# A context of 192 channels as a tile of 128 and a doubled tile of 64, with both ends of a fused transformer block reordered

## The reference

```python
B, N, D, H, DH, DC = 4, 512, 256, 16, 64, 192
def _attn(xq, ctx, wq, wkv, wo, bo):
    q = _heads(xq @ wq)
    k, v = jnp.split(ctx @ wkv, 2, axis=-1)
    q, k = _rope(q), _rope(_heads(k))
    a = jax.nn.softmax(jnp.einsum('bhnd,bhmd->bhnm', q, k) * DH ** -0.5, axis=-1)
    o = jnp.einsum('bhnm,bhmd->bhnd', a, _heads(v))
    return merge(o) @ wo + bo
attn_in = _adaln(x, cond, ...)
x = _attn(attn_in, attn_in, sa_wq, sa_wkv, sa_wo, sa_bo) + x
x = _attn(_adaln(x, cond, ...), _ln(context), ca_wq, ca_wkv, ca_wo, ca_bo) + x     # context: 192 channels
h = gelu(_adaln(x, cond, ...) @ ff_w1 + ff_b1)
x = h @ ff_w2 + ff_b2 + x
```

## Time and profile before

| | before |
|---|---|
| median of 3 runs | 1115.08 us (1114.47 to 1115.96) |
| profiled execution | 1118.88 us, its span 1117.1 us |
| TensorE matmul busy | 1097.2 us of the span (98%) |
| DVE, POOL, ACT busy | 858.1, 775.7, 636.9 us |
| mean granted TensorE clock | 0.994 of full speed |

### The profile page before, as it was taken

The page is one execution under the profiler, slowest core; times in us unless marked ns, Lnnn a source line. Parts: engine busy times, 40 slices in busy tenths (PEclk is TensorE's granted clock), DMA queues, the critical chain, the costliest instruction groups (busy, mean ns, idle before and its releaser), DMA issues.

```text
span 1117.1 us, 18312 instructions
## 1 busy us (share of the span) xinstructions
PE 1097.2 (98%) x6904; PEld 785.1 (70%) x6904; DVE 858.1 (77%) x1023; ACT 636.9 (57%) x895; POOL 775.7 (69%) x503
## 2 busy tenths in 40 slices
PE   8989999999999999999999999999999999989998
PEld 7657666776666776666766667766666776756997
DVE  5878887878787777878888777777877777788554
ACT  6465565665666555577665555555555545775521
POOL 2687887787788767789799766777777667755210
PEclk9899999999999999999999999999999999999999
DMA  6312121311231111211121112211121111300001
GB/s 175 86 46 57 32 53 39 89 30 30 53 77 38 39 36 23 72 39 39 29 63 38 39 39 59 51 23 36 38 72 39 37 31 30 114 1 1 20 19 38
DMA packets 59606, 52.31 MB, mean 47 GB/s; under 512 B 23040, under 2 KB 42496, under 8 KB 59264
## 3 DMA queue, kind: packets, MB, share of 16 engines
q1 hardware_dynamic: 57632, 49.57, 18.5%
q10 hardware_dynamic: 1888, 1.59, 0.5%
HBM read 15.22 MB, written 2.10 MB: 16 GB/s over the span
## 4 chain that ended last, share of the span: by engine, by line
PE 90%; DVE 5%; ACT 2%; issue 1%; DMA 1%; SPq 0%; POOL 0%; ACTq 0%; POOLq 0%; DVEq 0%
PE ps L872 18%; PE ps L713 12%; PE ps L715 11%; PE ps L714 11%; PE ps L813 6%; PE ps L860 6%; PE ps L848 5%; PE ps L819 5%; PE ps L815 5%; PE ps L817 5%; PE ps L963 4%; DVE lo L1083 1%; PE ps L729 1%; DMA x<-x_dram 1%; DVE w_lo L1117 1%
## 5 line engine op out<-in xcount | busy, mean ns | idle before, releaser
L548 ACT ACTIVATE probs<-ps 128x1024 f32<-128x1024 f32 x256 | 262.5, 1027 | 208.0 <-PE ps L819 183.6
L1065 DVE TENSOR_REDUCE neg_max<-ps 128x2 f32<-128x1024 f32 x256 | 301.6, 1226 | 76.7 <-PE ps L848 76.7
L420 POOL TENSOR_TENSOR acc<-acc,probs 128x1024 f32<-128x1024 f32 x128 | 306.2, 2392 | 18.6 <-POOL acc L415 0.4
L872 PE MATMUL ps<-probs,v 128*64 128x512 f32 x1024 | 230.7, 592 | 0.0
L415 POOL TENSOR_TENSOR acc<-probs 128x1024 f32<-128x1024 f32 x64 | 153.2, 2394 | 72.1 <-ACT probs L548 72.1
L872 PEld LDWEIGHTS ps<-probs,v 128*64 128x64 f32 x1024 | 73.9, 137 | 146.1 <-issue 146.1
L429 POOL TENSOR_TENSOR eo<-tmp 128x512 f32<-128x512 f32 x63 | 89.7, 1424 | 120.2 <-DVE tmp L1092 120.1
L1092 DVE TENSOR_TENSOR tmp<-ps,rope 128x1024 f32<-128x1024 f32 x126 | 148.2, 1211 | 4.5 <-PE ps L715 4.3
L813 PE MATMUL ps<-max_rows,pick 64*128 64x512 f32 x512 | 109.3, 419 | 2.6 <-DVE o_lo L1079 1.6
L713 PE MATMUL ps<-xn_hi,w_hi 128*128 128x512 f32 x256 | 107.8, 421 | 2.5 <-DVE o_lo L1079 1.3
L848 PE MATMUL ps<-hi 64*128 64x512 f32 x512 | 104.8, 400 | 5.4 <-DVE neg_max L1065 2.6
(11 more groups left out here) (116 smaller groups left out, 2250.0 us busy)
## 6 DMA issues: line engine op xcount, KB each, us to landing
lo<-eo SPq DMA_DIRECT2D x126, 256.0 KB, 3.2
w_raw<-pack_dram SPq DMA_DIRECT2D x16, 192.0 KB, 3.9
x<-x_dram SPq DMA_DIRECT2D x4, 512.0 KB, 7.5
w_raw<-pack_dram SPq DMA_DIRECT2D x8, 256.0 KB, 4.3
max_rows<-neg_max SPq DMA_DIRECT2D x128, 2.0 KB, 2.0
w_raw<-w_dram SPq DMA_DIRECT2D x2, 1024.0 KB, 5.8
out<-x SPq DMA_DIRECT2D x8, 256.0 KB, 2.2
ctx_in<-ctx_dram SPq DMA_DIRECT2D x4, 384.0 KB, 4.2
```

Of the source, the lines that this page charges most:

```text
L420: pool.tensor_tensor(acc[:, g % 2, :, :], acc[:, g % 2, :, :], probs[:, i, :, :], ALU.add).then_inc(added, 1)
L548: act.activation(probs[:, i, :, :], score_ps(i), ACT.Exp, scale=SCALE).then_inc(exped, 1)
L872: mm = pe.matmul(av_ps[DH * h:DH * h + DH, :], v[:, u % 2, kt, c:c + DH], probs[:, kt, h, :], start=(kt == 0), stop=(kt == TT - 1))
L1065: dve.tensor_reduce(neg_max[:, g % 2, :, i], peak_ps(i), AX.X, ALU.max, negate=True).then_inc(maxed, 1)
```

## The change

- **Context rows.** The 192 channels become one tile of 128 rows and a rest of 64 rows that is held twice, on partitions 0 to 63 and 64 to 127 (weights: four DMAs in place of two for each half, `LOADS` 5, 7 becomes 5, 11; the layer norm's rows: one more ACT instruction of 64 columns per token tile; its weights: four DMAs from SP in period 3 and a small ACT copy in period 5).
- **Keys** of the cross-attention (`is_rest`: even jobs from 32 on, periods 28 to 58): the rest as three pairs of matmuls, one on either half of the array, ahead of `total` (`project_rest`), which waits for the third maximum of that period; then six matmuls of 128 rows in the old place. Their banks are 4 and 5 in place of 3 and 4, and the first half of the output goes to bank 3.
- **Values** of quads 16 to 31: 12 matmuls of 128 rows, and the rest as six pairs at the period's end (`project_v_rest`). For quads 16 to 30 (`is_wide`) token tiles 0 and 2 go to banks 6 and 7, 1 and 3 to banks 2 and 5; ACT copies the first two, DVE the others, behind its rotates and `low_qk`. `left_in` replaces `side_free` and also guards banks 2 and 3 ahead of the second key tile's scores.
- **Start.** Job 3 is projected in four parts between and behind the peaks of pair 0. `low_qk(1)` goes from DVE in period 0 to POOL ahead of the loop, in front of `rotate(2)`. ACT's second high part goes ahead of `guess_rstd(2)`. The biases of the first layer move from periods 0, 1, 5, 7 to 13, 15, 18, 21.
- **End.** The weighted values of pair 61 get bank 5, so the scores of pair 62 don't wait for bank 1. DVE's `split_ffw` is one instruction for each matrix, W1's moves from behind `low_o` to in front of `normalise` in period 62. Statistics move ahead of `normalise` in period 61. DVE adds the last two exponentials of pair 63, in place of POOL's two additions.

```diff
         def v_ps(u, tt):
+            if is_wide(u):
+                return ps[:, ((6, 7), (2, 5))[tt % 2][tt // 2], 0:D]
...
+        def out_ps(u, r):
+            if u == QUADS - 1:
+                return last_ps[r]
+            return ps[:, (3 if is_job(2 * u + 6) and is_rest(2 * u + 6) else 5, 6)[r], :]
         def job_ps(j, e):
-            return ps[:, (0, 2)[e] if j == 2 else 3 + e, :]
+            return ps[:, (0, 2)[e] if j == 2 else (4 if is_rest(j) else 3) + e, :]
...
-        bias_in.update({0: 0, 1: 1, 5: 2, 7: 3})
+        bias_in.update({13: 0, 15: 1, 18: 2, 21: 3})
...
@@ gpsimd
                 if is_pair(p):
                     add_probs(p, 1)
-                    add_probs(p, 2)
-                    add_probs(p, 3)
+                    if p < PAIRS - 1:
+                        add_probs(p, 2)
+                        add_probs(p, 3)
...
             refine_rstd(pool, 2)
+            pool.wait_ge(qk_high, 2)
+            pool.tensor_tensor(lo[:, 1, :, :], raw_qk[:, 1, :, :], hi[:, 1, :, :], ALU.subtract).then_inc(qk_low_1, 1)
             rotate(2)
@@ scalar
                 if p in v_in:
                     keep_v(v_in[p], 0)
-                    keep_v(v_in[p], 1)
+                    if not is_wide(v_in[p]):
+                        keep_v(v_in[p], 1)
@@ tensor
+            def project_rest(j):
+                w, b, _ = quad(j // 2)
+                pe.wait_ge(maxed, 4 * (j - 3) + 3)
+                pe.wait_ge(w_split, 4 * w + 1)
+                pe.wait_ge(ln_split, 2 * norm_of(C, 1, b) + 2)
+                for n, (w_, a_) in enumerate(((w_hi, ctx_hi), (w_hi, ctx_lo), (w_lo, ctx_hi))):
+                    for e, half in enumerate(halves):
+                        c = slice(256 + e * 128, 256 + (e + 1) * 128)
+                        pe.matmul(job_ps(j, e), w_[half, 1, c], a_[half, b, 1, :], start=(n == 0), stop=False)
...
+            def project_v_rest(u):
+                b = quad(u)[1]
+                for t in range(2):
+                    for n, (a_, w_) in enumerate(((ctx_hi, w_hi), (ctx_hi, w_lo), (ctx_lo, w_hi))):
+                        for r, half in enumerate(halves):
+                            cut = slice((2 * r + t) * 128, (2 * r + t + 1) * 128)
+                            mm = pe.matmul(v_ps(u, 2 * r + t), a_[half, b, 1, cut], w_[half, 2, 256:512],
+                                           start=False, stop=(n == 2), skip_group_check=True)
+                            if n == 2 and (t == 1 if not is_wide(u) else r == 1):
+                                mm.then_inc(v_projected, 1)
...
+            def left_in(p, banks):
                 u = p // 2
                 if p % 2 == 0 and is_quad(u - 1):
+                    for r in range(2):
+                        if (3 if is_job(p + 4) and is_rest(p + 4) else 5, 6)[r] in banks:
+                            pe.wait_ge(o_added, 2 * (u - 1) + r + 1)
                 if p in v_in:
+                    held = ((6, 7), (2, 5)) if is_wide(v_in[p]) else ((3,), (4,)) if v_in[p] == QUADS - 1 else ((5,), (6,))
+                    for part in range(2):
+                        if any(bank in banks for bank in held[part]):
+                            pe.wait_ge(v_kept[part], v_in[p] + 1)
...
             def period(p):
+                if is_job(p + 4) and is_rest(p + 4):
+                    project_rest(p + 4)
                 if is_pair(p - 1):
                     total(p - 1)
...
+                if p in v_in and quad(v_in[p])[2] == 1:
+                    project_v_rest(v_in[p])
...
             modulate(3)
+            project_3(0, 0)
             peak(0, 2)
+            project_3(0, 1)
             peak(0, 3)
+            project_3(1, 0)
+            project_3(1, 1)
             norm(2, 0)
             norm(2, 1)
-            project(3)
@@ vector
                     for i in range(TT):
                         peak(p + 1, i)
-                if p == 0:
-                    low_qk(1)
+                if p == PAIRS - 3:
+                    norm_stats(stats_in[p])
+                if p == PAIRS - 2:
+                    split_ffw(0)
                 if is_pair(p - 1):
                     normalise(p - 1)
+                if p == PAIRS - 1:
+                    add_last_probs()
...
-                if p == PAIRS - 2:
-                    for c in range(4):
-                        split_ffw(0, c)
...
+                if p in v_in and is_wide(v_in[p]):
+                    keep_v(v_in[p])
                 if p % 2 == 0 and is_quad(u - 1):
                     add_out(u - 1, 0)
                     add_out(u - 1, 1)
```

More of the change, by code:

```diff
@@ L183, in build @@
         v_projected = sem("v_projected")
-        v_kept = sem("v_kept")
+        v_kept = [sem(f"v_kept{r}") for r in range(2)]
         scored = sem("scored")
@@ L504, in norm_rows @@
                 for tt in range(TT):
-                    act.activation(z[:, tt, 0:KT * rows], src[:, tt, :], ACT.Identity, bias=centre[:, tt:tt + 1],
+                    if order[n][0] == C:
+                        act.activation(z[:, tt, DC:D], src[:, tt, 128:DC], ACT.Identity, bias=centre[:, tt:tt + 1],
+                                       scale=rstd[:, tt:tt + 1])
+                    act.activation(z[:, tt, 0:src.shape[-1]], src[:, tt, :], ACT.Identity, bias=centre[:, tt:tt + 1],
                                    scale=rstd[:, tt:tt + 1]).then_inc(ln_rows, 1)
@@ L735, in project @@
                 w, b, phase = quad(u)
-                pe.wait_ge(w_split, 4 * w + place[k] + 1)
-                pe.wait_ge(ln_split, 2 * norm_of(C if k == 1 and phase == 1 else X, phase, b) + 2)
-                if k == 1 and phase == 1:
-                    rows, a_hi, a_lo = CK, ctx_hi, ctx_lo
-                else:
-                    rows, a_hi, a_lo = 128, xn_hi, xn_lo
-                for e in range(2):
-                    if j in (1, 3):
-                        pe.wait_ge(roped, 2 * (j - 1) + e + 1)
-                    if j == 3 and e == 1:
-                        pe.wait_ge(maxed, 3)
-                    for kt in range(KT):
+                whole = not is_rest(j)
@@ L748, in project @@
+                if whole:
+                    pe.wait_ge(w_split, 4 * w + place[k] + 1)
+                    pe.wait_ge(ln_split, 2 * norm_of(X, phase, b) + 2)
+                a_hi, a_lo = (xn_hi, xn_lo) if whole else (ctx_hi, ctx_lo)
+                for e in range(2):
+                    if j == 1:
+                        pe.wait_ge(roped, e + 1)
+                    for kt in range(KT if whole else 1):
                         c = slice(kt * 256 + e * 128, kt * 256 + (e + 1) * 128)
-                        mm = parts(job_ps(j, e), w_hi[0:rows, k, c], w_lo[0:rows, k, c],
-                                   a_hi[0:rows, b, kt, :], a_lo[0:rows, b, kt, :], kt == 0, kt == KT - 1)
+                        mm = parts(job_ps(j, e), w_hi[:, k, c], w_lo[:, k, c], a_hi[:, b, kt, :], a_lo[:, b, kt, :],
+                                   whole and kt == 0, not whole or kt == KT - 1)
@@ new lines, in project_v @@
+            def project_v(u):
+                w, b, phase = quad(u)
+                pe.wait_ge(w_split, 4 * w + 3)
+                if u == 0:
+                    pe.wait_ge(rope_kept, 1)
+                a_hi, a_lo = (ctx_hi, ctx_lo) if phase == 1 else (xn_hi, xn_lo)
+                for tt in (0, 2, 1, 3) if is_wide(u) else range(TT):
+                    cut = slice(tt * 128, (tt + 1) * 128)
+                    first = is_wide(u) or tt % 2 == 0
+                    for kt in range(1 if phase == 1 else KT):
+                        c = slice(kt * 256, (kt + 1) * 256)
+                        for n, (a_, w_) in enumerate(((a_hi, w_hi), (a_hi, w_lo), (a_lo, w_hi))):
+                            mm = pe.matmul(v_ps(u, tt), a_[:, b, kt, cut], w_[:, 2, c],
+                                           start=first and kt == 0 and n == 0, stop=(phase == 0 and kt == KT - 1 and n == 2),
+                                           skip_group_check=True)
+                    if phase == 0 and tt % 2 == 1:
+                        mm.then_inc(v_projected, 1)
@@ L858, in total @@
                     pe.wait_ge(o_added, 2 * (QUADS - 1))
+                    pe.wait_ge(last_added, 1)
                 for h in range(2):
-                    mm = pe.matmul(sum_ps(g)[DH * h:DH * h + DH, :], ones[:, :], acc[:, g % 2, h, :], start=True, stop=True)
+                    out = sum_ps(g)[DH * h:DH * h + DH, :]
+                    mm = pe.matmul(out, ones[:, :], acc[:, g % 2, h, :], start=True, stop=g < PAIRS - 1)
+                    if g == PAIRS - 1:
+                        mm = pe.matmul(out, ones[:, :], tmp[:, 0, h, :], start=False, stop=True)
                 mm.then_inc(summed, 1)
@@ L1150, in period @@
                 if p == PAIRS - 2:
-                    for c in range(4):
-                        split_ffw(1, c)
+                    split_ffw(1)
             norm_stats(0)
```

173 lines of the change are left out of this document (103 added, 70 removed).

## The result

The changed kernel takes 1123.84 us (median of 5 runs, 1122.51 to 1125.16), against 1115.64 for the kernel before in the same comparison (5 runs, 1114.47 to 1118.14): ratio 1.0072, 95% interval 1.0058 to 1.0086. It is slower, by about 8 us. I had forecast 1111.1 with a range from 1101 to 1118. The profiled execution took 1124.07 us (span 1122.3), 5.2 more than that of before (1118.88, span 1117.1). In all comparisons on record the executions of the kernel before lie in two groups, 44 of 67 from 1114.4 to 1116.4 and 23 from 1117.6 to 1119.5, and the profiled one is of the upper group, which is why the traces differ by 5.2 where the medians differ by 8.2.

What follows compares the result with a forecast made beforehand. TensorE, busy 98% of the span, was taken as the bound while DVE keeps up. Terms -10.8 - 2.2 + 8.1 - 1.5 + 0.2 + 2.2 = -4.0 took 1115.08 to 1111.1 us, range 1101 to 1118.

Steps and rivals of the forecast that it cites:

- Values, -10.8: Values' 24 matmuls become 12 and six pairs, 0.12 each: 0.72 us less a period over 15 odd periods.
- rival 3: Half-height pairs of 256 columns in the values' rest do not run together: slower, 1122.6 us, chance 0.13.
- Keys, -2.2: 16 even periods: keys stream 0.55 us less, the third maximum's wait takes 0.41, leaving 0.14 a period.
- In other odd periods the copy ends about 0.1 in time.: DVE's copy of values outside periods 31, 33 and 59: ends about 0.1 us in time, no cost counted.
- Extra waits, +8.1: Contention of DVE with POOL, and peaks waiting for the values' copy behind `low_qk`: together 8.1 us more.
- The weight splits' 0.2 each: Six even periods with a weight split of about 1.3 on POOL: 0.2 us more each, 1.2 in all.
- ACT's extra instructions, 0: 16 more short ACT instructions lie in ACT's idle time at no cost; at most 9 us without that cover.
- Start, -1.5: First score at 45.0, not 43.23, but DVE waits in periods 0 and 1 go: -1.5 us, between -4 and +3.
- Biases, +0.2: Moved biases take two POOL contentions away and bring two: +0.2 us, bounded by 1.0 either side.
- End, +2.2: From period 60's values on, W1's low part ahead of `normalise` delays the second hidden block: +2.2 us, between -3 and +5.
- From the trace to the median: Profiled execution, 1118.88 us, stood 3.8 above the median of the runs; both were taken to keep their distance.
- the biases of 30: Period 30, where the bias addition now comes ahead of DVE's `low_qk`: 1.6 us more.

Runs made afterwards that it cites:

- experiment 4: Changed kernel with the three pairs for the keys' rest moved behind the weighted values, no longer ahead of the sums: 1116.87 us.
- experiment 11: Changed kernel with values' banks swapped, second context DMA, W1's low part behind the output's, keys' rest behind weighted values, pair 1's low part on DVE: 1100.33 us.
- experiment 1: Changed kernel with the two halves of the wide values swapping banks, so DVE's half, copied last, lies in banks 6 and 7: 1116.0 us.
- experiment 6: Changed kernel with the doubled 64 context channels loaded by a second DMA, so ACT's layer norm is one instruction per token tile: 1122.37 us.
- experiment 9: Changed kernel with the four bias additions of the first layer back in periods 0, 1, 5 and 7: 1123.83 us.
- experiment 8: Changed kernel with the low part of q and k of pair 1 back from POOL to DVE in period 0: 1120.7 us.
- experiment 7: Changed kernel with W1's low part back behind the low part of the output in period 62, still one instruction: 1118.95 us.
- experiment 5: Changed kernel with the keys' rest as six single matmuls on 64 rows in the old place, not three pairs ahead of the sums: 1133.39 us.
- experiment 3: Changed kernel with DVE's copy of the values ahead of the low part of q and k in periods 31, 33 and 59: 1121.18 us.
- experiment 2: Changed kernel with ACT copying both halves of the wide values in their old banks, DVE none: 1121.18 us.

## Why the prediction was wrong, point by point

The sum put two terms at nothing that weren't: the values' copy on DVE, said to end 0.1 in time, cost 0.33 us in each of 11 steady even periods, and ACT's short instructions, said to lie in its idle time, cost 2.8 us in four periods. It also missed period 36 and half clock behind two waits, and carried a distance from the trace to the median that did not last. The gains of the thinner values and keys themselves came as forecast.

- **Values, -10.8.** Right. Pairs of 256 columns run 0.12 apart, and rejecting rival 3 was right too, though the time it gave (1122.6) is near the one measured: its mechanism was absent. From the first value matmul to the next score it takes 2.33 in place of 2.97 (842.91 to 845.24, 777.90 to 780.87), and the step to the second score, in the even period, 0.23 in place of 0.35: 0.76 in all, against 0.72. The price of the change of tile shape did move from the scores to the rest pairs, as forecast.
- **Keys, -2.2.** Right in the steady periods. From the last peak to the first output it takes 0.18 less, against 0.14. The step to the rest pairs is 0.33 over the pace (0.56 where 0.23 is usual), against the 0.41 that I took. The later sums also hold the first output until its low part is done, just in time (the step behind it is 0.22 where 0.12 is usual, in all traces with the rest ahead of the sums, and 0.12 in experiments 4 and 11). With the rest behind the weighted values (experiments 4 and 11) that stretch is 7.14 to 7.16, so what hangs on the third maximum takes back 0.28.
- **"In other odd periods the copy ends about 0.1 in time."** This is the step that failed most, for its many repetitions, and the reason why a steady even period did not shrink. The copy costs 0.33 in each of the 11 steady even periods from 38 on (3.7 us, experiment 1), since it is made of the last matmuls of the period, begins 0.2 into the next one and holds the bank that is wanted first. The margin was within the error of my reckoning, and I set it to nothing and not to a bound.
- **Extra waits, +8.1.** Periods 32 and 34 came as forecast in place and cause: 2.0 and 3.9 longer, against 0.8 and 3.9. The match in period 34 is in part luck: the wait is 2.68 against 2.8, but 1.3 of the 3.9 is the lower clock behind it, where I had 1.1 for the bias addition. Period 36 did not: 1.6 longer, against 0.2. There DVE's low part stood beside POOL's additions, took 3.42 (601.43 to 604.85), and the rotations and the copy were queued behind it. The output additions of 28 and 30 cost 0.2 and 0.4, not 0.1 and 1.6. The weight splits' 0.2 each did not come: periods 38, 44, 46, 52 and 54 are at most 0.1 longer than their neighbours.
- **ACT's extra instructions, 0.** Wrong: 2.8 us in four periods, of which 0.9 comes back in periods 15 and 19, and 1.5 by the medians (experiment 6). I named ACT's idle share as cover, but what counts is what stands behind these instructions in the same period: the high part of the output, then its low part on DVE, then the output on TensorE.
- **Start, -1.5.** Right within its bounds: -2.1, with the first score at 45.1 (forecast 45.0) and 6.67 idle (forecast some 6). Some 1.9 of the gain is that of the moved biases in period 1 (experiment 9), which I had booked in the next item. The delay by the low part on POOL was in the forecast at 3.7, and experiment 8 gives 3.5.
- **Biases, +0.2.** Right in sum (experiment 9: no difference), wrong in size by place: 1.9 gained in period 1, 1.2 lost in periods 2 to 27.
- **End, +2.2.** Right in its mechanism, output 30 held by W1's split ahead of `normalise`; measured 3.3 with period 60's wait, against 2.7. The half clock behind the wait (1.4) was missing, in this place and in period 34. The other edits of the end were not taken apart.
- **From the trace to the median.** I took the median to keep its distance of 3.8 below the profiled execution. After the change the profiled execution stands 0.2 above the median. In the trace I missed 1124.07 by 9.2; the other 3.5 of the 12.7 come from this step. The 3.8 was that of one execution and no property of the kernel to be carried over. Which stretch of it was longer than in others isn't known.

In the trace the 9.2 are then: start -0.6, periods 2 to 27 +3.1, periods 28 to 37 +2.9, periods 38 to 59 +3.4, end +0.6 (sum 9.4, by rounding). The largest parts are two small costs that I had set to nothing because something seemed to cover them, 3.7 for the copy and 2.8 for ACT's instructions. Waits of periods 32 and 36 that were sized too small (1.2 and 1.4) and the lower clock behind two waits (1.3 and 1.4) come next, and terms that were sized too large (the biases of 30, the weight splits) take some of it back.

## What to carry to other kernels

Where a buffer is split between two engines, give the half that is made last to the bank that is read last: the same work in swapped banks was worth 7.8 us here. Cover is what stands ahead of the deadline in the same engine's queue, not the engine's idle share; an instruction put ahead of a chain is paid in full once the chain ends just in time. Time the edits of such a change one by one: here five small edits turned 0.7% slower into 1.45% faster, and two more made it 1.6%.

## What the runs showed of the hardware that I had not expected

- **The clock after a wait of 2 to 3.6 us can go either way in the same kernel.** Ahead of pair 32 TensorE waited 2.07 in the changed kernel and 2.06 in experiment 7, with the same instructions before and behind. The two timelines, as changed and of the experiment, and the granted clock behind the wait in the same order:

```profile
540.84 0.62 PE L952 MATMUL ps<-hi 64*128 64x512 f32 x2 [2.07 <-DVE v L1231]
```

```profile
541.20 0.82 PE L952 MATMUL ps<-hi 64*128 64x512 f32 x2 [2.06 <-DVE v L1231]
```

```profile
540.80:543.30 2.50, 2.46 (x20) 2.42 (x22) 1.80 (x2) 0.86 (x1) 1.67 (x2) 1.00 0.00 0
```

```profile
541.20:543.70 2.50, 2.50 (x12) 2.30 (x14) 1.23 (x1) 0.00 (x0) 1.60 (x2) 0.55 0.00 0
```

  Period 32 took 17.95 in the one and 19.59 in the other: 1.6 us for the same wait. Behind waits of 2.68, 3.61 and 6.67 the changed kernel's clock was at the lower level each time (1.2 of 2.4 GHz), at once or within 0.7 us. But behind the same 2.68 ahead of pair 34 the granted clock was 1.00 in the traces of experiments 6 and 9 (period 34 took 18.56 and not 19.86), and behind 3.60 in period 62 it was 1.00 in experiment 5 (17.9, against 19.6 here and 20.4 in experiments 1 and 3). Behind 6.65 to 6.69 it was 0.50 in all seven traces that have such a wait; behind those of 1.1 to 1.5 us in the loop it stayed at 1.00 in the changed kernel and in experiments 1 to 9 (in the kernel before it was 0.63 behind one of 1.7 that had followed another of 1.54). So a wait of 2 to 3.6 us has to be booked at its length and at 0 to 2.5 us more. My estimate from these is that single profiles of such a kernel differ by 1 to 3 us for this alone.
- **Some DVE instructions and POOL's take turns by whole instructions**, also where DVE's is tiny: 128 x 4 elements took 1.88 us until POOL's addition ended (experiment 3), and W1's low part took 4.26 ahead of `normalise`, beside POOL's additions, and 2.36 in its place of experiment 7. The Trainium skill, "GPSIMD Engine Reference", section "8. Key points", says that the two share SBUF interfaces; the traces agree, and give the price as the rest of the instruction that runs.
- **A change between tiles of 128 and 64 rows costs 0.2 us** (experiment 5; and 844.21, 844.42, 844.64 above, where 0.12 is the pace), half ahead of the first matmul and half behind it. The Trainium skill, "TensorE: Matmul & The Clock Gate", section "Part 3: Packing small matmuls — row/col tiling", would have had successive pairs on the same row groups wait for their weight loads. The pairs 0.12 apart contradict it here; what costs is the change of shape.
